# Rebuilding the prologue of a graph attention layer with a routed FFN: order of loads, grouped normalisation, another step table

## The reference, cut to what matters

```python
xn = _layernorm(x, axis=-1)
x = x + _L0_gnn_ref(xn, edge_index, W, attn_l, attn_r, bias) + _L0_mix_ref(xn[None], W_qkv, b_qkv, W_out, b_out)[0]
x = x + _L0_ffn_ref(_layernorm(x, axis=-1)[None], Wr, br, W1, b1, W2, b2, gamma, beta)[0]

# in _L0_gnn_ref: 8 heads of 32 channels
h = (x @ W).reshape(n, HEADS, OUT_C)
a1 = jnp.sum(h * attn_l, axis=-1)
a2 = jnp.sum(h * attn_r, axis=-1)
e = jax.nn.leaky_relu(a1[src] + a2[dst], negative_slope=NEG_SLOPE)
ex = jnp.exp(e - seg_max[dst])
alpha = ex / segment_sum(ex, dst)[dst]
out = segment_sum(h[src] * alpha[:, :, None], dst)
```

## Time and profile before

| | us |
|---|---|
| median of 3 runs | 2740.4 |
| lowest and highest | 2737.08, 2741.24 |
| profiled execution, device time | 2743.08 |
| its span in the trace | 2741.3 |

### The profile page before, as it was taken

The page is one execution under the profiler, slowest core; times in us unless marked ns, Lnnn a source line. Parts: engine busy times, 40 slices in busy tenths (PEclk is TensorE's granted clock), DMA queues, the critical chain, the costliest instruction groups (busy, mean ns, idle before and its releaser), DMA issues.

```text
span 2741.3 us, 37518 instructions
## 1 busy us (share of the span) xinstructions
PE 2075.5 (76%) x8314; PEld 1415.2 (52%) x8315; DVE 1748.8 (64%) x3633; ACT 876.4 (32%) x1856; POOL 1672.4 (61%) x1764
## 2 busy tenths in 40 slices
PE   3777777777777777777777778788788773799997
PEld 2545545454554444455445455555555541477776
DVE  7566666666666666666666667777777667333334
ACT  1533333333333333333333332222222221433332
POOL 4177777777777777777777777777777771000000
PEclk9877888888788888887887878888878866899999
DMA  6655555555555555555555555555555551100000
GB/s 217 241 151 144 152 149 143 144 151 147 145 149 149 143 144 152 149 143 147 149 147 144 152 146 156 161 161 162 162 154 160 143 133 25 31 18 17 17 17 25
DMA packets 182669, 359.19 MB, mean 131 GB/s; under 512 B 39635, under 2 KB 92715, under 8 KB 182636
## 3 DMA queue, kind: packets, MB, share of 16 engines
q0 software_dynamic: 82848, 233.35, 32.0%
q1 hardware_dynamic: 98116, 123.87, 14.9%
q10 hardware_dynamic: 1672, 1.59, 0.2%
HBM read 325.91 MB, written 32.75 MB: 131 GB/s over the span
## 4 chain that ended last, share of the span: by engine, by line
PE 37%; issue 16%; DVE 16%; DMA 12%; ACT 11%; POOL 5%; DVEq 1%; SPq 0%; POOLq 0%; ACTq 0%
DMA work<-h_tab,idx 12%; PE bank L892 10%; PE bank L1005 6%; POOL work L579 5%; ACT work L676 5%; PE bank L995 4%; PE bank L901 4%; DVE zs L1270 4%; PE bank L910 3%; DVE acc L1300 2%; DVE zb L1272 2%; DVE zb L1273 2%; DVE zb L1271 2%; PE bank L899 1%; PE bank L944 1%
## 5 line engine op out<-in xcount | busy, mean ns | idle before, releaser
L579 POOL DMA_INDIRECT work<-h_tab,idx x1712 | 1626.0, 950 | 525.2 <-issue 444.0
L892 PE MATMUL bank<-work 128*128 128x264 f32 x3424 | 1074.0, 464 | 311.3 <-DVE acc L1300 304.7
L892 PEld LDWEIGHTS bank<-work 128*128 128x128 f32 x3424 | 729.0, 227 | 566.1 <-DVE acc L1300 408.2
L1292 DVE TENSOR_TENSOR work<-work,bank 128x1024 f32<-128x1024 f32 x428 | 520.4, 1216 | 168.7 <-issue 154.6
L1300 DVE TENSOR_TENSOR acc<-bank,acc 128x264 f32 x854 | 366.1, 429 | 285.4 <-PE bank L892 277.4
L684 ACT ACTIVATE bank<-zb 128x64 f32<-128x64 f32 x214 | 48.7, 228 | 1457.1 <-DVE zb L1275 1453.2
L1185 DVE TENSOR_TENSOR work<-bank,cols 128x1024 f32<-128x1024 f32 x215 | 261.1, 1215 | 0.0
L678 ACT ACTIVATE work<-work,ones 128x1024 bf16<-128x1024 bf16 x215 | 246.8, 1148 | 7.0
L676 ACT ACTIVATE work<-work,pcol 128x1024 bf16<-128x1024 bf16 x215 | 243.5, 1132 | 6.4 <-DMA work<-dst_d 6.4
L606 POOL COPY work<-acc 128x768 f32 (+2 forms) x17 | 13.6, 805 | 368.7 <-PE bank L957 295.8
L1270 DVE TENSOR_REDUCE zs<-bank 128x128 f32<-128x384 f32 x214 | 118.2, 552 | 165.7 <-DMA work<-h_tab,idx 165.2
(11 more groups left out here) (241 smaller groups left out, 1903.6 us busy)
## 6 DMA issues: line engine op xcount, KB each, us to landing
work<-dst_d SPq DMA_DIRECT2D x216, 256.0 KB, 3.8
work<-h_tab,idx POOLq DMA_INDIRECT x1712
xx_d<-acc SPq DMA_DIRECT2D x49, 256.0 KB, 2.1
xnt_c<-xx_d SPq DMA_DIRECT2D x66, 128.0 KB, 3.6
h_tab<-acc SPq DMA_DIRECT2D x49, 132.0 KB, 1.9
xn_c<-xx_d SPq DMA_DIRECT2D x49, 128.0 KB, 2.3
q2t_d<-q2t_c SPq DMA_DIRECT2D x49, 128.0 KB, 1.9
X<-x SPq DMA_DIRECT2D x6, 1024.0 KB, 11.9
```

The source lines that it names most:

```text
L579: nc.gpsimd.indirect_dma_start(out=ring[q][:, j, :], out_offset=None, in_=h_tab, in_offset=bass.IndirectOffsetOnAxis(ap=idx[:, q, j:j + 1] ...
L892: ins = mm(bank[3 + s % 2][:, 0:TW], hot[q][:, s * G + g, :], ring[q][:, s * G + g, :], start=(g == 0), stop=(g == G - 1))
L1292: v.tensor_tensor(m, m, ex, ALU.mult).then_inc(msg_ready, 1)
```

## The change

It touches the prologue and the first pass.

- SP issues the first eight tiles of x (two halves) ahead of the last destinations, which now come in two DMAs instead of seven.
- DVE starts with `wg`, then the statistics of tiles 0 to 7, then the reduces over W_qkv. Each later group of eight tiles is measured during the group ahead of it: bn_stats in its tiles 0 to 3, `ln_var` in tile 4, the root on ACT after its tile 5, `ln_root` after tile 7 (`LN`, `LN_AT`).
- The step table is made in three pieces inside the first pass, `lows` after tile 1, `pasts` after tile 4, `units` after tile 7. `below` compares the 806 last destinations with the 49 tile starts; PE counts (at tile 3) how many units lie below each tile, which gives the first step of each tile; `past` compares the step numbers with those 49 values, and PE counts again (at tile 6), which gives the tile of each step. The unit of a step is its number less that count, plus one. The rows `t_acc` and `t_a2c` now come straight from PSUM and lie on partitions 0 and 32 of one tensor.
- POOL corrects W_qkv ahead of the 14 table gathers instead of after them. The zero fill of the accumulator moves from POOL to ACT. POOL no longer waits for the stores of xn.
- The first pass is written out for all 49 tiles on all engines. `convert` is at tile 30, the transposes of chunks at tiles 33 to 35.
- The 16 attention columns are copied out in one copy; the maximum is then taken from `a2c`.
- The banks that a step's messages go to are now a list of two, `MB = [3, 4]`, with the same order as before.

```diff
+        LN = [(g * A1, g * A1 + A1) for g in range(NT // A1)] + [(NT - 1, NT)]
+        LN_AT = [g * A1 + 5 for g in range(NT // A1)]
         TT = 3
-        TA = A1 * Q_MID
+        T_CONVERT = 30
+        T_TURN = T_CONVERT + 3
...
+            HX = XC // 2
+            sp.dma_start(X[:, 0:HX, :], xv[:, 0:HX, :]).then_inc(x_loaded[0], 16)
+            sp.dma_start(X[:, HX:XC, :], xv[:, HX:XC, :]).then_inc(x_loaded[7], 16)
             sp.wait_ge(lastd_clear, 1)
-            for c in range(UCH):
-                n = min(P, U - c * P)
-                sp.dma_start(lastd[0:n, c:c + 1], dst[c * P:c * P + n, EG - 1:EG],
-                             allow_slow_non_contiguous=True).then_inc(lastd_loaded, 16)
-            for c in range(6):
+            sp.dma_start(lastd[:, 0:UF], dst[0:UF * P, EG - 1:EG].rearrange("(c p) o -> p (c o)", p=P),
+                         allow_slow_non_contiguous=True).then_inc(lastd_loaded, 16)
+            sp.dma_start(lastd[0:U - UF * P, UF:UCH], dst[UF * P:U, EG - 1:EG],
+                         allow_slow_non_contiguous=True).then_inc(lastd_loaded, 16)
+            for c in range(1, 6):
...
+                if t == T_CONVERT + 2:
+                    sp.wait_ge(dst_kept, 1)
+                    sp.dma_start(dst_d.rearrange("(c p) e -> p c e", p=P), b_dst).then_inc(dst_stored, 16)
...
+            nc.gpsimd.iota(kcol.bitcast(I32), pattern=[[P, KCH]], base=0, channel_multiplier=1).then_inc(iota_set, 1)
+            nc.gpsimd.iota(tlow.bitcast(I32), pattern=[[P, NT]], base=0, channel_multiplier=0).then_inc(iota_set, 1)
             nc.gpsimd.iota(iotai, pattern=[[1, KS]], base=0, channel_multiplier=0).then_inc(iota_set, 1)
-            nc.gpsimd.iota(kcol.bitcast(I32), pattern=[[P, KCH]], base=0, channel_multiplier=1).then_inc(iota_set, 1)
-            nc.gpsimd.iota(uio.bitcast(I32), pattern=[[P, UCH]], base=0, channel_multiplier=1).then_inc(iota_set, 1)
-            nc.gpsimd.memset(acc[:, A_COLS:], 0.0).then_inc(acc_zero, 1)
-            pool.wait_ge(ucol_ready, 1)
...
+            pool.wait_ge(ucol_ready, 1)
+            for c in range(KCH):
...
-            for stored in (h_stored, xx_stored):
-                all_stored(pool, stored)
+            all_stored(pool, h_stored)
...
-            root(0, rstd[:, 0:TA])
+            act.wait_ge(lastd_clear, 1)
+            nc.scalar.copy(acc[:, A_COLS:], small[:, 31:32].to_broadcast([P, NT * TW - A_COLS])).then_inc(acc_zero, 1)
...
+                if t in LN_AT:
+                    g = LN_AT.index(t) + 1
+                    root(g, rstd[:, LN[g][0]:LN[g][1]])
...
+            act.wait_ge(dst_stored, 16)
...
-            pe.wait_ge(cmp_done, 1)
-            for c in range(KCH):
-                mm(bank[6][:, c:c + 1], cmp[:, c * P:(c + 1) * P], ones[:, 0:1], start=True, stop=True)
-            for k in range(2):
-                ins = mm(bank[7 - k][0:1, 8:8 + KS // 2], ones[:, 0:1], cmp[:, k * (KS // 2):(k + 1) * (KS // 2)],
-                         start=True, stop=True)
-            ins.then_inc(u_counted, 1)
...
+                if t == 3:
+                    pe.wait_ge(below_ready, 1)
+                    for c in range(UCH):
+                        ins = mm(bank[7][0:NT, 480:481], below[:, c, :], ones[:, 0:1], start=(c == 0), stop=(c == UCH - 1))
+                    ins.then_inc(tiles_counted, 1)
+                if t == 6:
+                    pe.wait_ge(past_ready, 1)
+                    for c in range(KCH):
+                        mm(bank[7][:, ROW + c:ROW + c + 1], past[0:NT, c * P:(c + 1) * P], ones[0:NT, 0:1], start=True, stop=True)
+                    for r, k in enumerate(ROWS):
+                        ins = mm(bank[k][0:33, 0:ROW], ones[0:NT, 0:33], past[0:NT, r * ROW:(r + 1) * ROW], start=True, stop=True)
+                    ins.then_inc(steps_counted, 1)
...
-            dve.wait_ge(lastd_loaded, 16 * UCH)
-            dve.wait_ge(lastd_clear, 1)
-            own(v.tensor_scalar(lastt, lastd, 7, None, ALU.arith_shift_right))
-            own(v.tensor_scalar(fcol, lastt, float(NT - 1), None, ALU.min))
-            own(v.tensor_tensor(fcol, fcol, tcol[:, 0:UCH], ALU.add))
-            own(v.tensor_scalar(cmp, kio, fcol[:, 0:1], None, ALU.is_gt))
-            for c in range(1, UCH):
-                ins = v.scalar_tensor_tensor(out=cmp, in0=kio, scalar=fcol[:, c:c + 1], in1=cmp, op0=ALU.is_gt, op1=ALU.add)
-                own(ins)
-            dve.sem_inc(cmp_done, 1)
...
-            dve.wait_ge(u_counted, 1)
-            v.tensor_scalar(ucol, bank[6][:, 0:KCH], float(U), None, ALU.min).then_inc(dve_own, 1)
-            own(v.tensor_copy(urow[0:1, 0, 0:KS // 2], bank[7][0:1, 8:8 + KS // 2]))
...
+            dve.wait_ge(x_loaded[0], 16)
+            for t in range(A1 // 2):
+                measure(t)
+            dve.wait_ge(x_loaded[7], 16)
+            for t in range(A1 // 2, A1):
+                measure(t)
+            dve.wait_ge(x_measured, A1)
+            ln_var(own, *ln_of(0))
             dve.wait_ge(w_loaded, 16 * NW)
-            own(v.tensor_copy(bvx, bv_col[:].unsqueeze(2).to_broadcast([P, KC, P])))
-            dve.sem_inc(bvx_ready, 1)
+            v.tensor_reduce(small[:, 0:4].rearrange("p (k a) -> p k a", a=2),
+                            wqkv[:, :, 0:2 * C].rearrange("p k (a n) -> p k a n", a=2), AX.X, ALU.add).then_inc(w_summed, 1)
+            v.tensor_reduce(small[0:1, 4:6], bqk[:], AX.X, ALU.add).then_inc(w_summed, 1)
+            ln_root(own, 0, rstd[:, 0:A1])
...
+            def lows():
+                dve.wait_ge(iota_set, 3)
+                v.tensor_copy(iota_p[:], iotai[:, 0:P])
+                v.tensor_copy(kio, iotai).then_inc(dve_own, 1)
+                own.n += 1
+                own(v.tensor_copy(ucol, kcol.bitcast(I32)))
+                v.tensor_scalar(pcol[:], ucol[:, 0:1], -1.0, None, ALU.mult)
+                v.tensor_scalar(kcol, ucol, 1.0, None, ALU.add)
+                v.tensor_copy(tlow, tlow.bitcast(I32))
+                dve.wait_ge(lastd_loaded, 32)
+                own(v.tensor_copy(lastf, lastd))
+                v.tensor_tensor(below, lastf.unsqueeze(2).to_broadcast([P, UCH, NT]),
+                                tlow.unsqueeze(1).to_broadcast([P, UCH, NT]), ALU.is_lt).then_inc(below_ready, 1)
+            def pasts():
+                dve.wait_ge(tiles_counted, 1)
+                own(v.tensor_tensor(first[0:NT], bank[7][0:NT, 480:481], ucol[0:NT, 0:1], ALU.add))
+                v.tensor_scalar(past[0:NT, :], kio[0:NT, :], first[0:NT], None, ALU.is_ge).then_inc(past_ready, 1)
+            def units():
+                dve.wait_ge(steps_counted, 1)
+                count = bank[7][:, ROW:ROW + KCH]
+                own(v.tensor_tensor(kcol, kcol, count, ALU.subtract))
+                v.tensor_scalar(ucol_i, kcol, float(U), None, ALU.min).then_inc(ucol_ready, 1)
+                v.tensor_scalar(tcol, count, -1.0, float(P), ALU.add, ALU.mult).then_inc(dve_own, 1)
+                own.n += 1
+                for r, k in enumerate(ROWS):
+                    v.tensor_scalar(t_acc[:, r * ROW:(r + 1) * ROW], bank[k][0:1, 0:ROW], -1.0, float(TW), ALU.add, ALU.mult)
+                    ins = v.tensor_scalar(t_a2c[:, r * ROW:(r + 1) * ROW], bank[k][32:33, 0:ROW], -1.0, float(PARTS * AW),
+                                          ALU.add, ALU.mult)
+                own(ins)
+                dve.sem_inc(t_ready, 1)
...
+                g = n + 1
+                if t < NT - 1:
+                    if p == 0:
+                        dve.wait_ge(x_loaded[g], 16)
+                    if g < NT // A1 and p < A1 // 2:
+                        measure(g * A1 + 2 * p)
+                        measure(g * A1 + 2 * p + 1)
+                    if g == NT // A1 and p == 0:
+                        measure(NT - 1)
+                    if p == A1 // 2:
+                        dve.wait_ge(x_measured, min((g + 1) * A1, NT))
+                        ln_var(own, *ln_of(g))
+                    if p == A1 - 1:
+                        ln_root(own, g, rstd[:, LN[g][0]:LN[g][1]])
+                if t == 1:
+                    lows()
+                if t == 4:
+                    pasts()
+                if t == 7:
+                    units()
+                if t == A1 + 1:
+                    dve.wait_ge(w_loaded, 16 * NW)
+                    own(v.tensor_copy(bvx, bv_col[:].unsqueeze(2).to_broadcast([P, KC, P])))
+                    dve.sem_inc(bvx_ready, 1)
+                if t == T_CONVERT:
                     convert()
-                if isinstance(t, int) and t == TA - A1:
-                    dve.wait_ge(w_loaded, 16 * NW)
-                    v.tensor_reduce(small[:, 0:4].rearrange("p (k a) -> p k a", a=2),
-                                    wqkv[:, :, 0:2 * C].rearrange("p k (a n) -> p k a n", a=2), AX.X, ALU.add).then_inc(w_summed, 1)
-                    v.tensor_reduce(small[0:1, 4:6], bqk[:], AX.X, ALU.add).then_inc(w_summed, 1)
```

(9 more changed lines are left out.)

175 lines of the change are left out of this document (69 added, 106 removed).

## The result

| | kernel before | changed kernel |
|---|---|---|
| median of 4 runs, us | 2740.82 (2737.08 to 2741.86) | 2721.60 (2719.78 to 2722.57) |
| profiled execution, us | 2743.1 | 2722.57 |
| its span, us | 2741.3 | 2720.8 |

The ratio is 0.9932, 95% interval 0.9914 to 0.9949: 19.2 us faster. The forecast was 2726.7, its range 2716 to 2737; the change gives 5.1 us more than forecast.

The account below looks back on a forecast made before the run. POOL's 1712 indirect gathers bound the edge loop, a fixed block, so only the first gather's start counts. Stretches of 18.7, 25.6, 59.9 and 6.6 put it at 110.8 against 124.5, 13.7 less: 2726.7 us, range 2716 to 2737.

Parts of the forecast that it names:

- The forecast case: Prologue: first gather 13.7 us earlier, loop unchanged, 2726.7 on the scale of the median; chance 0.60.
- The start: Prologue up to the first normalisation: loads, weights, statistics and W_qkv reduces sum to 18.7 us, bounds 17.8 to 22.
- the sharing of DMA: Initial loads: x shares the DMA engines with the weights, which land 0.9 us later.
- The port: Early first pass: DVE's small operations contend with POOL's W_qkv chain, charged 1.5 us over tiles 0 to 7.
- Tiles 0 to 7: First pass with the table: tiles, slow clock and serial DVE-PE round trips sum to 25.6 us, ending at 44.3.
- Tiles 8 to 48: Rest of first pass: 59.9 us, including 2.8 for five boundaries, 2.9 for conversion, 2.3 twice for the clock, 3.1 for chunks.
- The tail: From pass end to first gather: the same chain, 7.1 us, taken as 6.6 because DMA has more gaps.
- The loop: Edge loop from first to last gather: a block of fixed length, 2146.6 us, untouched by the change.
- B: First pass: PE's clock falls at every group boundary, costing 10 us; gain only 3.7, time 2737; chance 0.13.
- A: First pass: table work hides in PE's slow first tiles and the clock stays up; 10.6 more gain, 2716; chance 0.14.
- C: First pass: DMA becomes the pace, so the time stays the same, 2740; chance 0.08.
- D: First pass: code of 33 more unrolled tiles arrives late; at 0.6 us per tile 2747, slower; chance 0.05.

Follow-up runs that it names:

- third group: Both kernels unchanged, rerun on one chip: 2739.2 for the kernel before, 2721.8 for the changed kernel, ratio 0.9938.
- first profile: Changed kernel as profiled in the first comparison with the kernel before: 2722.57 us, first gather at 108.6.
- by the experiment: Zero fill moved back from ScalarE to POOL in the changed kernel: 3236.7 us, changed kernel there 3230.2.
- the experiment's last round: Changed kernel with SP's stores of tiles 16 to 31 and 40 to 47 looped again, the last loop a single round: 3233.0 us.
- the later table: Changed kernel with counts' compare at tile 6, unit numbers at 10, four table rows at 13 to 15: 3218.8 and 3225.1 us, ratios 0.9911 and 0.9899.
- the other kind of chip: Changed kernel, unchanged, on chips where the kernel before took 3247.9 and 3257.9 us: 3228.0 and 3230.2, ratios 0.9938 and 0.9907.
- the table and conversion spread: Changed kernel with table answers later and index conversion spread over tiles 29 to 42: 3219.5 and 2707.9 us, ratios 0.9885 and 0.9886.

## Why the prediction was nearly right, step by step

The forecast case came true, with a gain of 13.7 from the prologue forecast and 15.9 measured (17.0 in the third group), and a loop that is the same block. That the total is so near is in part luck: in the first profile the first two stretches came out 1.0 and 2.2 longer than forecast, the last two 3.0 and 2.4 shorter. Its parts, in us, between the same cuts:

| stretch | forecast | first profile | third group |
|---|---|---|---|
| to the first normalisation | 18.7 | 19.7 | 19.0 |
| to the end of tile 7's matmuls | 25.6 | 27.8 | 25.8 |
| to the end of the pass | 59.9 | 56.9 | 57.6 |
| to the first gather | 6.6 | 4.2 | 4.4 |
| first gather at | 110.8 | 108.6 | 106.8 |

- **The start.** The term that was mis-sized is the sharing of DMA: 0.9 forecast. The weights' last load took 8.3 to landing against 6.4, 1.9; with the later issue DVE began at 10.18 instead of 9.0. The kernel with x behind the destinations shows the cause: 5.9 and 7.62. The rest, 9.7 by the sum, took 9.56. The normalisation at 19.74 lies inside the 17.8 to 22 named.
- **The port.** The charge of 1.5 under POOL's W_qkv chain was too high: the seven small operations and the compare beside it took 2.3 in all (21.71 to 24.0), against the 2.1 that I had put for them without it. The fill, which the change moved away, is what hurts: 3.1 to the first normalisation, by the experiment. I named the port for the wrong instruction.
- **Tiles 0 to 7.** The two trips are there, as waits of 1.35 and 3.68 at tiles 4 and 8, and moving their answers brought the first gather 6.4 and 6.6 us forward. What I had not in the sum is a fall of the clock behind the first of them: two tiles at 2.02 and 1.67. In the third group it did not come, and the stretch is 25.8, against the 25.6 of the sum. That agreement is in part luck: up to the end of tile 3 it was 1.2 shorter than my terms (the port's 1.5 was hardly there), the trip at tile 4 was 0.9 shorter, and against that tile 7 took 2.5 instead of 1.1, since its matmuls ran at the low clock that I had put behind it, and the step count and its trip took 0.9 more.
- **Tiles 8 to 48.** I had 2.8 for five boundaries. Four of them cost 0.4 each, 1.7: the fifth falls under the conversion's shadow, and the variances never showed. The clock behind the count and its trip cost 1.2 in this stretch (2.3 forecast), since tile 7 had its part already. The conversion's wait was 2.12, and with the refill behind it 2.3 (2.9 forecast); the clock behind it cost 1.7 from start to start of the matmuls (2.3 forecast). The index chunks took 3.6 (3.1 forecast). With 46.7 for the tiles themselves the sum is 57.2, 0.3 over the measured 56.9.
- **The tail.** The step that failed is "the same chain". I took 0.5 off for DMA; the real change was SP's backlog. The kernel before, in which L448 stores xn and L450 h:

```profile
117.81 0.39 ACT L654 COPY acc<-bank 128x272 f32<-128x272 f32 x1 [0.53 <-PE bank L816]
118.32 1.18 SPq L448 DMA_DIRECT2D xx_d<-acc  x1
120.63 0.44 SPq L450 DMA_DIRECT2D h_tab<-acc  x1
```

  Its last store is issued 2.4 after the last h copy has ended (118.20); in the changed kernel it is 0.2 after. The chain is 2.9 shorter, 7.1 to 4.2, and the backlog is 2.2 of it; another 0.5 lies between the last issue and the gather. The backlog of before grows over its loop: 0.16 at tile 18, 0.95 at tile 31, 1.60 at tile 46, 2.43 at tile 48, and within 0.07 of that in its profile of the third group. Each new round of the loop adds some 0.4, and 0.8 come at tile 47, where one store took 1.18 to issue instead of 0.33. What is once added stays, since the rolled pitch, 1.11 or 1.12 a pair, hardly gains on PE's 1.14, while the unrolled one, 1.00, does: the changed kernel is 1.14 behind at tile 42 and 0.52 at tile 46. That unrolling SP alone removes the backlog wasn't shown by a run: the experiment's last round wasn't rolled. I had costed the loops' registers at nothing because PE hides DVE, and didn't ask it of SP, which stands in the tail.
- **The loop.** Forecast as a fixed block of 2146.6, measured 2140.7. On this kind of chip the third group settles it: 2140.3 before, 2141.9 after. The block is the same in both; the 2146.6 came from a profile whose gathers took 949 ns instead of 946, and 1711 times 3 ns is 5 us, more than most terms of my sum. So 4.6 of the 20.5 us between the first two profiles were not the prologue's. That the median of the runs came out 5.1 beyond the forecast has two parts: the prologue gave 2.2 to 3.3 more than I had, and the rest isn't assigned.

The rivals: B, a fall at every boundary, did not come in any of the profiles: behind waits of 0.17 to 0.31 the matmuls kept 1.08. A, the table hides, is wrong for the change as it is; the later table shows what that would be worth, 6.4 to 6.6 at the first gather (7.0 to 9.0 at tile 9) where the rival said 10.6. The rest of it is the clock, which fell at the step count in the kernel with the later table all the same. C: DMA is full at the end (the share is 0.87 over the pass), but that was no bound: with the table and conversion spread the first gather moved 11.2 earlier. D: nothing on the first kind of chip; on the other kind PE, ACT and DVE stand still without a releaser in the pass, and the ratio is still 0.9938 and 0.9907.

## What to carry to other kernels

When a long fixed loop makes a change worth only what it moves the loop's start, take a second profile of the kernel before: a few ns on each of 1712 instructions outweigh the terms being argued. Take it on the same chip: here the gathers' duration went with the chip. Ask of each queue in the tail, SP's too, whether its own pitch is below the pace of what feeds it; what a loop adds to it is paid there. And an answer that two engines owe each other costs its full trip at the place where it is asked for: asking two or three tiles later, and handing its parts out over several tiles, brought 11 to 14 us here on top of the change's 17 to 19.
